# A decoder layer on one core: Wo behind the attention product, LayerNorm statistics behind v, row copies among the carries, expert gathers one by one, another order of the weight split

## The chip, the cores and the metric

One core of a Trainium2 chip runs the whole kernel in one launch. The metric is device time in microseconds (us), lower is better; times given are medians of several executions.

## The reference, cut to what matters

Input `x` is 16 sequences of 128 rows of 256 numbers. Three sublayers follow each other, each `x = x + f(LayerNorm(x))`:

```python
# 1: gated linear attention, 8 heads of 128; q, k normalised to length 1, alpha = sigmoid(x Wg)
S = a_t[..., None] * S + k_t[..., None] * v_t[:, :, None, :]     # one step of 128
o_t = einsum('bhkv,bhk->bhv', S, q_t)                             # then o @ Wo
# 2: cross attention to ctx: softmax(x (ctx W^T)^T) ctx
# 3: mixture of 8 experts, chosen per sequence (top 2 by the mean over its rows)
h = gelu(einsum('bsd,bkcd->bksc', x, Wd) + bd) * top_w            # Wd = down_w[top_i]: a gather
out = einsum('bksc,bkdc->bsd', h, Wu) + (top_w * bu).sum(1)
```

## The kernel before, in words

The 16 sequences are four groups `i` of four. A **unit** `n = 8 i + h` is the attention of one head `h` for one group, so there are 32 units. The recurrence over 128 steps is replaced by seven levels of a doubling scheme: `decay` (VectorE) and `carry` (ScalarE) make the operands of level l from those of level l-1, TensorE multiplies them (`levels`, in three runs: levels 0 and 2; 1, 3 and 4; 5 and 6), `keep` (VectorE) and `expand_*` (ScalarE) put the results into `attnT`, `attend` multiplies by v, `attend_transposed` turns the result, and `output_projection` adds it times Wo into an accumulator. Projections use float32 split into two parts, so `project` has three matmuls where one would do; the split of each weight is a cast on ScalarE and a subtraction on VectorE at the start (`split_weights`). Norms of q and k are sums of squares by 64 tiny matmuls (`norms`), floored by VectorE (`norm_floor`), raised to -1/2 by GpSimd (`reciprocal_norms`) and applied in `v_scaled` and `o_scaled`.

Sublayers 2 and 3 of group i-1, the **tail**, are woven into the units of group i. Each engine runs a list written out by hand; `tail_part(n, place)` puts a tail step at a head h and at a place in the unit. On TensorE the places are S (start), A (behind the second run of levels) and B (behind `attend`). On VectorE they are early, late, mid and end; on ScalarE early, mid and end. LayerNorm is `ln_variance` (VectorE), `ln_power` (GpSimd), `ln_normalize` (VectorE, writes `xn`), and then transposes of `xn` on TensorE: x2T for sublayer 2, x3T for sublayer 3, xT for the attention of the next group. Projections, v, o, transposes and tail products all go through four PSUM banks used in a fixed cycle (`ring`): a product waits until the one four places earlier has been read. The three long stretches in which tail and attention run together (units 8 to 15, 16 to 23, 24 to 31) are called passes 1, 2 and 3 here, units 0 to 7 pass 0. After unit 31 the tail of the last group runs by itself, in two halves.

Engines wait for each other by semaphores only; each engine works strictly in its own order, so a wait holds up all that is behind it. GpSimd also issues the four gathers of the chosen experts' weights (`fetch_experts`, one for each sequence of a group).

## Time and profile before

| | us |
|---|---|
| median of 3 runs | 564.17 (562.89 to 567.42) |
| profiled execution, its own time | 563.17 |
| its span | 561.4 |
| TensorE matmuls busy | 488.9 (87%) |
| VectorE busy | 383.1 (68%) |
| ScalarE busy | 356.9 (64%) |
| GpSimd busy | 85.1 (15%) |

The span is what the trace covers; the run's own time is 1.8 us longer. The granted clock of TensorE is a share of its full rate: 1.0 is 2.4 GHz, 0.5 is 1.2 GHz.

### The profile page before, as it was taken

What the parts mean: (1) busy time and instruction counts of PE and PEld (TensorE: products, weight loads), DVE (VectorE), ACT (ScalarE), POOL (GpSimd) and SP (SyncE); (2) the same over time, 40 slices, a digit from 0 to 9 for tenths busy, and PEclk for the clock granted to TensorE, in tenths of its full rate; (3) what the DMA queues carried; (4) which work ended last, traced back from release to release, by engine and by line L of the source; (5) the groups of instructions that cost most, each with busy time, mean ns of one, the idle gap of its engine ahead of it and who ended that gap; (6) DMA issues with size and microseconds to landing.
All of it is one profiled execution on the core that took longest, in us unless ns stands there. A gap on an engine that the chain in (4) does not pass through costs nothing. (4 is left out here: it accounts for less than half of the span.)

```text
span 561.4 us, 25935 instructions
## 1 busy us (share of the span) xinstructions
PE 488.9 (87%) x11232; PEld 407.4 (73%) x11232; DVE 383.1 (68%) x1069; ACT 356.9 (64%) x825; POOL 85.1 (15%) x71
## 2 busy tenths in 40 slices
PE   1798999999988999899988999899988999775616
PEld 1587888888877888787867888688867887664415
DVE  4588887766786888765686887765775888614541
ACT  4667787766758677567758677577748676442202
POOL 1012111111111111410111111410111111300020
PEclk9999999999999999899999999899989999997557
DMA  8800000001010100210010100210000100201021
GB/s 334 252 3 5 4 4 4 4 4 40 4 41 2 41 4 4 77 41 22 23 40 5 40 4 4 78 40 22 23 2 4 40 5 4 78 0 39 0 75 37
DMA packets 15264, 20.35 MB, mean 36 GB/s; under 512 B 1200, under 2 KB 12976, under 8 KB 15152
## 3 DMA queue, kind: packets, MB, share of 16 engines
q1 hardware_dynamic: 13872, 14.49, 7.6%
q0 software_dynamic: 1280, 4.20, 2.6%
q8 instruction: 89, 1.46, 1.1%
q14 instruction: 23, 0.19, 0.1%
HBM read 16.60 MB, written 2.10 MB: 33 GB/s over the span
## 5 line engine op out<-in xcount | busy, mean ns | idle before, releaser
L438 ACT COPY states<-states 128x512 f32<-128x512 f32 (+1 forms) x160 | 94.6, 592 | 95.3 <-DVE states L646 88.6
L363 POOL TENSOR_TENSOR rnorm<-norm_sq,neg_half 128x8 f32<-128x8 f32 (+1 forms) x33 | 53.8, 1631 | 291.0 <-DVE norm_sq L686 291.0
L646 DVE TENSOR_TENSOR states<-states,spans 128x512 f32<-128x512 f32 x128 | 88.5, 691 | 12.2 <-DVE states L646 4.6
L1128 PE MATMUL acc<-wo_sb,oT_sb 128*128 128x256 f32 x256 | 63.8, 392 | 8.2 <-ACT oT_sb L465 8.2
L1030 PE MATMUL ring<-xnT,wk_sb 128*128 128x512 f32 x192 | 55.7, 429 | 8.9 <-DVE v_sb L695 6.0
L1043 PE MATMUL ring<-wv_sb,xnT 128*128 128x256 f32 x384 | 57.5, 302 | 0.6 <-DVE wv_sb L877 0.6
L1128 PEld LDWEIGHTS acc<-wo_sb,oT_sb 128*128 128x128 f32 x256 | 46.0, 189 | 15.3 <-ACT oT_sb L465 9.3
L1030 PE MATMUL ring<-xnT,wq_sb 128*128 128x512 f32 x192 | 53.1, 412 | 1.7 <-ACT rowsT L469 1.0
L677 DVE COPY_PREDICATED blocks<-owned,lo_bank 128x128 f32<-128x128 uint32 x128 | 38.5, 301 | 20.2 <-PE lo_bank L1053 14.8
L1043 PEld LDWEIGHTS ring<-wv_sb,xnT 128*128 128x128 f32 x384 | 50.9, 200 | 1.1 <-DVE wv_sb L877 0.7
L1030 PE MATMUL ring<-xnT,wg_sb 128*128 128x512 f32 x192 | 51.0, 402 | 0.0
L1030 PEld LDWEIGHTS ring<-xnT,wk_sb 128*128 128x128 f32 x192 | 36.1, 200 | 16.8 <-DVE v_sb L695 7.1
L1030 PEld LDWEIGHTS ring<-xnT,wq_sb 128*128 128x128 f32 x192 | 33.6, 188 | 9.2 <-ACT rowsT L469 1.4
L1030 PEld LDWEIGHTS ring<-xnT,wg_sb 128*128 128x128 f32 x192 | 35.0, 195 | 6.2 <-DVE xnT L749 0.2
L460 ACT COPY attnT<-blocks 32x128 f32<-32x128 f32 x128 | 37.4, 292 | 1.1
L1109 PEld LDWEIGHTS ring<-v_sb,attnT 128*128 128x128 f32 x256 | 33.0, 192 | 5.2 <-issue 4.3
L450 ACT COPY attnT<-hi_bank 32x64 f32<-32x64 f32 x128 | 26.0, 203 | 16.0 <-PE hi_bank L1100 8.5
L1109 PE MATMUL ring<-v_sb,attnT 128*128 128x128 f32 x256 | 33.8, 275 | 0.4 <-issue 0.4
L1100 PE MATMUL hi_bank<-ones,squares 128*32 128x1 f32 x2048 | 26.7, 173 | 7.8 <-issue 5.9
L1100 PEld LDWEIGHTS hi_bank<-ones,squares 128*32 128x32 f32 x2048 | 24.2, 110 | 10.1 <-issue 7.9
L663 DVE TENSOR_TENSOR spans<-spans 128x128 f32<-128x128 f32 (+3 forms) x128 | 28.4, 222 | 4.4
L1053 PE MATMUL lo_bank<-states 128*32 128x32 f32 x2048 | 29.6, 198 | 1.5 <-issue 1.5
(145 smaller groups left out, 852.4 us busy)
## 6 DMA issues: line engine op xcount, KB each, us to landing
x_buf<-x_dram SPq DMA_DIRECT2D x4, 512.0 KB, 4.2
ctxT_sb<-ctxT_dram SPq DMA_DIRECT2D x8, 256.0 KB, 3.4
ctx_sb<-ctx_dram SPq DMA_DIRECT2D x4, 512.0 KB, 4.8
out_dram<-x_mid SPq DMA_DIRECT2D x8, 256.0 KB, 2.1
states<-wk_dram SPq DMA_DIRECT2D x1, 1024.0 KB, 6.1
states<-wg_dram SPq DMA_DIRECT2D x1, 1024.0 KB, 8.1
states<-wq_dram SPq DMA_DIRECT2D x1, 1024.0 KB, 10.1
v_sb<-wv_dram SPq DMA_DIRECT2D x1, 1024.0 KB, 11.7
```

The costliest lines, as they stand in the source:

```text
L363: nc.gpsimd.tensor_tensor(rnorm[:, m % 4, first:last], norm_sq[:, first:last], neg_half[:, first:last], ALU.pow).then_inc(rnorm_set, 1)
L438: nc.scalar.copy(dst, src).then_inc(carry_set, 1)
L460: last = nc.scalar.copy(attnT[lo:lo + BLOCK, :, lo:lo + BLOCK], blocks[lo:lo + BLOCK])
L646: nc.vector.tensor_tensor(dst, src, by, ALU.mult).then_inc(decayed, 1)
L663: nc.vector.tensor_tensor(spans[:, span_at(l):span_at(l) + m], view(src, off, [[2, m]]), view(src, off + 1, [[2, m]]), ALU.mult).then_inc( ...
L677: nc.vector.copy_predicated(blocks[:].rearrange("p b t -> p (b t)"), owned[:, mask].bitcast(U32), of_bank[:, N_IN * at:N_IN * at + N_IN]). ...
L1030: last = mm(dst[:], w[:, a, c, P * h:P * h + P], xnT[:, i % 2, b, c], start=(c == 0 and k == 0), stop=(c == KC - 1 and k == 2))
L1043: last = mm(dst[:, 2 * P * k:2 * P * k + 2 * P], xnT[:, i % 2, a, c, T * b:T * b + T], wv_sb[:, w, c, 2 * P * pair:2 * P * pair + 2 * P], ...
L1053: last = mm(dst[BLOCK * r:BLOCK * r + BLOCK, to:to + BLOCK], left[:, at:at + BLOCK], right[:, at:at + BLOCK], start=True, stop=True)
L1100: last = mm(hi_bank[BLOCK * r:BLOCK * r + BLOCK, to:to + 1], squares[:, a, at:at + BLOCK], ones[:], start=True, stop=True)
L1109: last = mm(dst[:, P * b:P * b + P], attnT[:, b], v_sb[:, n // 2 % 2, b, n % 2], start=True, stop=True)
L1128: last = mm(accs[z][:, D * m:D * m + D], oT_sb[:, n % 2, T * b:T * b + T], wo_sb[:, h], start=(h == 0 and m == 0), stop=(h == H - 1 and m ...
```

## The change

On TensorE, in each unit, `output_projection(n - 2)` moves from before place A to behind `attend(n - 1)`; x3T moves from S of head 5 to B of head 4. On VectorE, `residual` moves from mid to end of head 1 (behind `o_scaled`), `ln_variance("mid")` from end of head 1 to early of head 2 (behind `v_scaled`), and `weigh_up` from head 7 to head 0 of the next group. On ScalarE, the copies of x2T and probsT move to a new place between carries 2 and 3, and those of x3T from early of head 5 to end of head 4. On GpSimd, the power for q and that for k become two instructions with a semaphore each, and the gathers of a group are issued one at a time: sequence 0 in unit h = 6, sequence 1 when `norms` of that unit is done, sequences 2 and 3 behind the first and the second run of levels of unit h = 7. At the start the order is k 0, g 0, q 0, k 1 instead of k 0, k 1, g 0, q 0, and a one-column copy (`warm`) stands ahead of the first cast.

```diff
-            if place == "S" and h == 5 and t >= 0:
+            if place == "B" and h == 4 and t >= 0:
                 found = [("x3T", t, 0), ("x3T", t, 1)]
...
-            order = [("xT", 0, 0), ("xT", 0, 1), ("k", 0), ("k", 1), ("g", 0), ("q", 0)]
+            order = [("xT", 0, 0), ("xT", 0, 1), ("k", 0), ("g", 0), ("q", 0), ("k", 1)]
...
             def reciprocal_norms(m):
...
-                nc.gpsimd.tensor_tensor(rnorm[:, m % 4, first:last], norm_sq[:, first:last], neg_half[:, first:last],
-                                        ALU.pow).then_inc(rnorm_set, 1)
+                if m + 2 < U:
+                    nc.gpsimd.tensor_tensor(rnorm[:, m % 4, GB:2 * GB], norm_sq[:, GB:2 * GB],
+                                            neg_half[:, GB:2 * GB], ALU.pow).then_inc(rk_set, 1)
+                if m >= -1:
+                    nc.gpsimd.tensor_tensor(rnorm[:, m % 4, 0:GB], norm_sq[:, 0:GB], neg_half[:, 0:GB],
+                                            ALU.pow).then_inc(rq_set, 1)
...
             for n in range(U):
                 i, h = divmod(n, H)
+                if h == 7 and i > 0:
+                    pool.wait_ge(norm_mm, n + 2)
+                    fetch_experts(i - 1, (1,))
                 if 1 <= n:
                     reciprocal_norms(n - 1)
-                if h == 1 and i > 0:
+                if h == 2 and i > 0:
                     ln_power(("mid", i - 1))
...
                 if h == 6 and i > 0:
-                    fetch_experts(i - 1)
+                    fetch_experts(i - 1, (0,))
+                if h == 7 and i > 0:
+                    for run, b in ((RUNS[0], 2), (RUNS[1], 3)):
+                        pool.wait_ge(level_mm, LEVELS * n + DONE[run[-1]])
+                        fetch_experts(i - 1, (b,))
...
-                    if at == (2, "end"):
+                    if at == (2, "carry"):
                         for c in range(KC):
                             tail_to(rowsT[:, c], ("x2T", t, c), x2T_set)
                     if at == (3, "early"):
                         probs_out(t)
-                    if at == (3, "end"):
+                    if at == (3, "carry"):
                         tail_to(probsT[:].rearrange("p b t -> p (b t)"), ("probsT", t, 0), probsT_set)
-                    if at == (5, "early"):
+                    if at == (4, "end"):
                         for c in range(KC):
                             tail_to(rowsT[:, c], ("x3T", t, c), x3T_set)
...
-                if n + 1 < U:
-                    for l in range(1, INNER):
+                for l in range(1, INNER):
+                    if n + 1 < U:
                         carry(n + 1, l)
+                    if l == 2:
+                        tail_part(n, "carry")
                 tail_part(n, "end")
...
             act.wait_ge(consts_set, 1)
+            nc.scalar.copy(warm[:], neg_half[:, 0:1])
             split_weights(0)
             xT_upper(0)
             split_weights(1)
+            split_weights(2)
             k_out(0)
-            split_weights(2)
+            split_weights(3)
+            alpha_out(0)
+            q_out(0)
             k_out(1)
-            alpha_out(0)
-            split_weights(3)
-            q_out(0)
...
-                dve.wait_ge(rnorm_set, 2 * pair + 2)
+                dve.wait_ge(rk_set, 2 * pair + 2)
...
-                dve.wait_ge(rnorm_set, n + 2)
+                dve.wait_ge(rq_set, n + 1)
...
+                if at == (0, "late") and i >= 2:
+                    weigh_up(i - 2)
-                    if at == (1, "mid"):
+                    if at == (1, "end"):
                         residual(t)
-                    if at == (1, "end"):
+                    if at == (2, "early"):
                         ln_variance(("mid", t), x_mid)
...
-                    if at == (7, "late"):
-                        weigh_up(t)
...
             norm_floor(-2)
+            span_products(0)
             split_weights(3)
-            span_products(0)
...
                 if n < U:
                     levels(n, RUNS[1])
-                if n >= 2:
-                    output_projection(n - 2)
                 if n < U:
                     tail_part(n, "A")
                 if n >= 1:
                     attend(n - 1)
+                if n >= 2:
+                    output_projection(n - 2)
                 tail_part(n, "B")
```

TensorE around place A of head 2 (`L1128` before and `L1147` now are Wo, `L1137` and `L1156` the transposes of `xn`, `L1109` and `L1128` now `attend`). Before:

```order
L1053 MATMUL hi_bank<-states 32x32 x32
L1053 MATMUL lo_bank<-states 32x32 x16
L1128 MATMUL acc<-wo_sb,oT_sb 128x256 x4
L1137 MATMUL ring<-ident,xn 128x128 x8
L1109 MATMUL ring<-v_sb,attnT 128x128 x4
```

And now:

```order
L1072 MATMUL hi_bank<-states 32x32 x32
L1072 MATMUL lo_bank<-states 32x32 x16
L1156 MATMUL ring<-ident,xn 128x128 x8
L1128 MATMUL ring<-v_sb,attnT 128x128 x4
L1147 MATMUL acc<-wo_sb,oT_sb 128x256 x4
```

Wo stood between the levels and the transposes, and now stands behind the attention product.

VectorE from the end of unit h = 1 into unit h = 2. Before:

```order
L719 TENSOR_TENSOR x_mid<-acc,x_buf 128x512 x2
L710 TENSOR_TENSOR o_sb<-ring,rnorm 128x512
L612 BN_STATS stats<-x_mid 128x6 x4
L607 MEMSET scratch 128x1
L617 BN_AGGR mean_var<-stats 128x2 x4
L620 TENSOR_SCALAR var_eps<-mean_var 128x4
L686 TENSOR_SCALAR norm_sq<-hi_bank 128x8
L677 COPY_PREDICATED blocks<-owned,hi_bank 128x128 x2
L646 TENSOR_TENSOR states<-states,spans 128x2x16x16
L653 TENSOR_TENSOR states<-states,spans 128x4x32 x2
L695 TENSOR_TENSOR v_sb<-ring,rnorm 128x512
```

And now:

```order
L728 TENSOR_TENSOR o_sb<-ring,rnorm 128x512
L737 TENSOR_TENSOR x_mid<-acc,x_buf 128x512 x2
L704 TENSOR_SCALAR norm_sq<-hi_bank 128x8
L692 COPY_PREDICATED blocks<-owned,hi_bank 128x128 x2
L661 TENSOR_TENSOR states<-states,spans 128x2x16x16
L668 TENSOR_TENSOR states<-states,spans 128x4x32 x2
L713 TENSOR_TENSOR v_sb<-ring,rnorm 128x512
L627 BN_STATS stats<-x_mid 128x6 x4
L622 MEMSET scratch 128x1
L632 BN_AGGR mean_var<-stats 128x2 x4
L635 TENSOR_SCALAR var_eps<-mean_var 128x4
```

The statistics are computed behind the scaling of v; nothing was added or taken away.

GpSimd in heads 6 and 7 of pass 1, with the semaphores that each waits for. Before:

```order
L363 TENSOR_TENSOR rnorm<-norm_sq,neg_half 128x8 [waits v_set,o_set,norm_sq_set] x2
L370 DMA sel<-expert_dram,row_idx 128x513 [waits idx_set]
L370 DMA sel<-expert_dram,row_idx 128x513 x3
```

And now:

```order
L374 DMA sel<-expert_dram,row_idx 128x513 [waits idx_set]
L374 DMA sel<-expert_dram,row_idx 128x513 [waits idx_set,norm_mm]
L364 TENSOR_TENSOR rnorm<-norm_sq,neg_half 128x4 [waits v_set,o_set,norm_sq_set]
L367 TENSOR_TENSOR rnorm<-norm_sq,neg_half 128x4
L374 DMA sel<-expert_dram,row_idx 128x513 [waits idx_set,level_mm] x2
```

Four gathers in a row have become four that each wait for a point of TensorE's list.

## Rows read from the trace of the kernel before

**Rows 1.** Windows: us; busy PE, PEld, DVE, ACT, POOL; clock; DMA share; GB/s.

```profile
27.70:150.00 122.30, 120.88 (x3254) 100.94 (x3255) 91.68 (x235) 89.41 (x213) 17.91 (x11) 0.99 0.03 8
150.00:270.00 120.00, 112.76 (x2623) 94.93 (x2625) 89.62 (x257) 83.63 (x196) 20.45 (x15) 0.99 0.10 30
```

**Rows 2.** TensorE's waits: who waited for whom, us in total, times, longest.

```profile
PE acc L1128 <- ACT oT_sb L465: 8.2, 8, 2.9
PE ring L1030 <- DVE v_sb L695: 6.0, 3, 2.0
PE hi_bank L1100 <- issue: 5.9, 13, 0.5
...
PE ring L1146 <- issue: 3.3, 3, 1.2
...
PE ring L1030 <- ACT rowsT L469: 1.0, 3, 0.5
PE ring L1163 <- ACT probsT L469: 1.0, 2, 0.5
```

**Rows 3.** Timeline of the start: start us, us, engine, line, [idle before <- releaser].

```profile
7.93 1.28 ACT L528 ACT_TABLE_LOAD   x1 [7.93 <-DMA states<-wk_dram]
9.23 1.90 ACT L528 CAST wk_sb<-states 128x2048 fp32r<-128x2048 f32 x1
...
25.33 2.29 DVE L877 TENSOR_TENSOR wv_sb<-v_sb,wv_sb 128x2048 fp32r<-128x2048 f32 x1 [2.33 <-ACT wv_sb L528]
...
27.68 2.93 PE L1043 MATMUL ring<-wv_sb,xnT 128*128 128x256 f32 x12 [0.63 <-DVE wv_sb L877]
```

**Rows 4.** Timeline of heads 1 and 2 of pass 1, three engines.

```profile
154.09 1.28 DVE L719 TENSOR_TENSOR x_mid<-acc,x_buf 128x512 f32<-128x512 f32 x2
156.01 1.39 DVE L612 BATCH_NORM_STATS2 stats<-x_mid 128x6 f32<-128x256 f32 x4
158.11 1.01 POOL L355 TENSOR_TENSOR rstd<-var_eps,neg_half 128x4 f32<-128x4 f32 x1 [13.04 <-DVE var_eps L620]
160.89 0.69 DVE L695 TENSOR_TENSOR v_sb<-ring,rnorm 128x512 f32<-128x512 f32 x1 [1.00 <-issue]
163.55 1.38 DVE L628 TENSOR_SCALAR xn<-x_mid,mean_var,rstd 128x256 f32<-128x256 f32 x4
166.06 1.04 PE L1137 MATMUL ring<-ident,xn 128*128 128x128 f32 x8
```

**Rows 5.** Timeline of head 3 of pass 1: the normalisation for the next group, and Wo.

```profile
180.97 1.38 DVE L628 TENSOR_SCALAR xn<-x_buf,mean_var,rstd 128x256 f32<-128x256 f32 x4
181.35 1.99 PE L1128 MATMUL acc<-wo_sb,oT_sb 128*128 128x256 f32 x8 [0.90 <-ACT oT_sb L465]
```

**Rows 6.** Timeline of head 3 of pass 0: the same two.

```profile
70.49 1.38 DVE L628 TENSOR_SCALAR xn<-x_buf,mean_var,rstd 128x256 f32<-128x256 f32 x4
70.98 2.00 PE L1128 MATMUL acc<-wo_sb,oT_sb 128*128 128x256 f32 x8
```

**Rows 7.** Timeline: the end of a unit without a gather beside it.

```profile
140.55 0.73 PE L1100 MATMUL hi_bank<-ones,squares 128*32 128x1 f32 x64
141.21 1.68 PE L1043 MATMUL ring<-wv_sb,xnT 128*128 128x256 f32 x12
```

**Rows 8.** Timeline: the end of unit h = 6 of pass 1, beside the gathers.

```profile
229.12 0.62 PE L1100 MATMUL hi_bank<-ones,squares 128*32 128x1 f32 x12
...
232.26 2.93 PE L1043 MATMUL ring<-wv_sb,xnT 128*128 128x256 f32 x12
...
234.99 1.82 PE L1030 MATMUL ring<-xnT,wg_sb 128*128 128x512 f32 x6
```

**Rows 9.** Windows of 1 us: columns as in the first group.

```profile
231.00:232.00 1.00, 0.51 (x26) 0.43 (x29) 0.87 (x6) 0.00 (x0) 0.41 (x1) 1.00 0.64 213
233.00:234.00 1.00, 1.00 (x7) 1.00 (x6) 0.10 (x1) 0.96 (x5) 0.00 (x0) 0.50 0.37 140
```

**Rows 10.** The chain that ended last: start us, us, what (the last gather of the kernel).

```profile
542.67 3.85 DMA sel<-expert_dram,row_idx
```

More of the change, by code:

```diff
@@ L357, in reciprocal_norms @@
             def reciprocal_norms(m):
-                first, last = (4 if m < -1 else 0), (8 if m + 2 < U else 4)
                 pool.wait_ge(norm_sq_set, m + 3)
@@ L362, in reciprocal_norms, with fetch_experts @@
                 positive(pool, v_set, m - 1)
-                nc.gpsimd.tensor_tensor(rnorm[:, m % 4, first:last], norm_sq[:, first:last], neg_half[:, first:last],
-                                        ALU.pow).then_inc(rnorm_set, 1)
-            def fetch_experts(t):
+                if m + 2 < U:
[4 more added lines that the diff above has]
+                                            ALU.pow).then_inc(rq_set, 1)
+            def fetch_experts(t, sequences):
                 pool.wait_ge(idx_set, t + 1)
                 positive(pool, out_set, 2 * t)
-                for b in range(GB):
+                for b in sequences:
                     nc.gpsimd.indirect_dma_start(
@@ L392, in _ @@
                                         ALU.pow).then_inc(half_rstd[z], 1)
-            fetch_experts(NG - 1)
+            fetch_experts(NG - 1, range(GB))
         @block.scalar
@@ L918, in _ @@
                 tail_part(n, "end")
+            tail_part(U, "late")
             for k in range(LO_KEPT, KEEPS):
@@ L1241, in _ @@
             project(wk_sb, ("k", 0)).then_inc(k_mm, 1)
-            project(wk_sb, ("k", 1)).then_inc(k_mm, 1)
-            norms(-2)
             pe.wait_ge(w_split, 2)
             project(wg_sb, ("g", 0)).then_inc(g_mm, 1)
+            norms(-2)
             pe.wait_ge(w_split, 3)
             project(wq_sb, ("q", 0)).then_inc(q_mm, 1)
+            project(wk_sb, ("k", 1)).then_inc(k_mm, 1)
             norms(-1)
```

10 lines of the change are left out of this document (7 added, 3 removed).

## The prediction

> **What bounds the kernel now.** I read the windows of the span first, then TensorE's waits, then the timeline where those waits stand. The reader is to see in the windows [rows 1] that TensorE is the bound: in pass 0 it works 120.9 of 122.3 us, so nothing on VectorE (91.7) or ScalarE (89.4) can matter there, while in a window of a pass with a tail it works 112.8 of 120.0. The 7 us between are the prize, three times. The list of waits [rows 2] says what they are: Wo waiting for ScalarE's copy of oT (8.2 us in 8 waits), project k waiting for a ring bank that VectorE's scaling of v frees (6.0 in 3), the norms matmuls stopping for nothing that the profile shows (5.9 in 13 pieces), scores for its row copies (3.3 in 3), and 1.0 each for the copies of x3T and probsT. Each of the five edits aims at one of these. The question for each is what is late next on an engine that works in order.
>
> **Start.** A table load of 1.28 stands ahead of the first cast, which starts at 9.23 [rows 3]; a tiny copy ahead of it takes the load to where ScalarE is idle anyway. The v projection of unit 0 starts at 27.68, right behind the subtraction for wv (25.33 to 27.6), before which VectorE waited 2.33 for the cast of wv. That cast now comes before alpha, so the wait goes, but VectorE now waits for alpha and does the span products first. Lower bound 1.3 (the table load alone), upper 1.28 + 2.33 = 3.6. Besides, that first v projection ran at half clock, 2.93 against 1.68 in steady state [rows 3, 7], behind a TensorE with gaps; starting with fewer gaps may save the 1.25. Bounds 1.3 and 4.9; I take **3.0**, in the middle, since neither part is excluded. All of it counts, because TensorE bounds pass 0.
> The Trainium skill, ScalarE: Activation LUTs, section What ACT_TABLE_LOAD costs, puts a switch at about 1.28 us of load plus 1.38 of drain. The cast here starts 0.02 behind the end of the load [rows 3], so no drain is seen; by the page the start would return 1.4 us more.
>
> **Pass 0, head 3.** Wo, 2.0 long, started at 70.98, and the normalisation that the transposes of place A need ended at 70.49 + 1.38 = 71.9 [rows 6]: Wo covered it. With Wo behind `attend`, the transposes come first and wait 0.9. Nothing gives it back: **-0.9**.
>
> **Head 2 of each pass.** Before, the statistics (from 156.01 until GpSimd's power at 158.11, 2.1 us) and then a wait of 1.00 behind that power put the scaling of v at 160.89 [rows 4]; k waited 2.0 for it. Now the residual (1.28) only changes places with `o_scaled`, and the scaling of v comes 2.1 + 1.0 earlier, at about 157.8: k's wait is gone. The split power helps here: q and k apart take 1.01 each (the row of four columns), and v needs the first alone. But the statistics are still to be done before x2T. From scaling v to normalising took 163.55 - 160.89 = 2.66; with the statistics between, normalising starts at 157.8 + 2.66 + 2.1 = 162.6 and ends at 164.0. TensorE finished its levels at 166.06 less one Wo of about 1.85, that is 164.2, and without k's wait would at 162.2. Place A, formerly behind Wo, now comes at once: x2T waits 1.8. So 2.0 are gained and 1.8 lost: a wait of the same size, for the same VectorE work, 6 us later. **+0.5** for the three.
>
> **Head 3 of passes 1 and 2.** x2T's row copies between the carries are ready before scores asks, 3.3 / 3 = 1.1 gained. TensorE finished its levels at 181.35 - 0.90 = 180.4 [rows 5], now 1.3 earlier, 179.1, and does probsT (0.4). The xT transposes then need `xn`, which is ready at 180.97 + 1.38 = 182.35 and is bound by ScalarE's and VectorE's own chain, not by TensorE: a wait of 2.8. Then transposes 0.9, `attend` 1.0, Wo 1.85: 186.1, where the old order came to 183.2 + 0.4 + 0.9 + 1.0 = 185.5 and then waited 0.5 for probsT. The gains of scores (1.1), Wo (0.9) and probsT (0.5) are all spent on this wait: **0**. Pass 3 has no next group, no xT, and keeps them: 1.1 + 0.9 + 0.3 = **+2.3**.
>
> **x3T** in place B of head 4 needs an `xn` that is ready, with Wo ahead of it; its three waits go: **+1.0**. ScalarE does the two copies before `expand_wide` instead of behind it, the same work where it waited for norms anyway.
>
> **Other Wo waits.** 8.2 less the three of 0.9 in head 3 is 5.5. The last (about 0.7) has nothing to hide behind; of the 2.9 the `attend` now ahead waits for ScalarE's blocks written just before, so only 0.5 comes back; the remaining 1.9 (ScalarE late after table loads) is hidden by `attend` and keys. **+2.4**.
>
> **Gathers.** Undisturbed, norms take 140.55 to 141.21, 0.7 us; beside the four gathers 229.12 to 232.26, 3.1 [rows 7, 8]. In the window of 231 TensorE works half the time while the DMA engines are 0.64 busy; at 233 its clock is 0.50, 1.2 GHz, and v takes 2.93 (v to g 2.73 against 1.5) and g 1.8 [rows 8, 9]. Cost: 2.4 + 1.2 + 0.3 = 3.9. Pass 2 is alike, and pass 3 has the 2.4 without the slow clock: 10.2. My reading: instructions are fetched by DMA, 64 tiny matmuls use them up fast, and gather packets delay them. One by one, gathers 1, 2 and 3 go out at points behind which TensorE has long matmuls; gather 0 still falls near the norms. I leave 0.5 a pass for it and 0.3 for short unit 31: **+8.4**, bounds 0 (the stalls have another cause, or follow the gathers) and 10.2.
> The Trainium skill, Runtime: NRT & Kernel Launch, section Instruction fetch mechanics, says that a sequencer refills itself in blocks of 16 KiB and that this is mostly hidden. By that rule the stalls were not fetches and spreading gathers would return nothing; that is the first rival.
>
> `weigh_up` goes from head 7 to head 0, where its product is needed only after `attend` and Wo; VectorE is 1.2 later with its carries there and waits for the up products afterwards anyway: 0.
>
> **Clock.** The new waits of 1.8 to 2.8 (five of them) can bring the half clock, as the 2.4 of scattered idling did; of the three old k waits of 2.0 I cannot exclude it either. One more event of 1.2: **-1.2**; bounds 0 and 5 x 1.5 = 7.5.
>
> **Sum.** 3.0 - 0.9 + 0.5 + 2.3 + 1.0 + 2.4 + 8.4 - 1.2 = 15.5. The profiled execution took 563.17 (span 561.4), 1.0 under the median of 564.17; 563.2 - 15.5 = 547.7, so **548**.
>
> **Rivals.**
> - *The norms' stalls stay.* For: their releaser is unnamed, and small ones occur elsewhere without gathers. Against: three bursts, each exactly at the gathers, the DMA share rising with them. Then 548 + 8.4 = 556. Chance 0.20.
> - *Cold waits.* Each long wait at place A halves the clock for some 3 us. For: the clock after the gathers [rows 9]. Against: k's three waits of 2.0 stand in windows whose mean clock is 0.99 [rows 1]. 548 + 6 = 554. Chance 0.09.
> - *Better*: the start's upper end, all gather stalls gone, no slow clock: 542. Chance 0.08.
> - *Slower: the last gather.* It is issued behind the second run of levels of head 7; TensorE then has keys, `attend` and Wo, about 1.7 + 1.0 + 1.85 = 4.6 us, before the transposes of the gathered weights, and all of TensorE is queued behind these. From issue to landing the last gather took 3.85 [rows 10], so it fits by 0.7. Beyond 4.6 each us costs 3 (three passes); from 9.8 us on the change is slower than before, and at 12 it is 548 + 22 = 570. For: the gather shares GpSimd with the powers. Against: 3.85 was measured right behind three others. Chance 0.04.
> - *The edits do little*, because waits fall on other engines that I took for slack: 560. Chance 0.04.
>
> My forecast has 0.55, within 545 to 551. The range **541 to 558** takes in the upper end of the start, the full 10.2 for gathers, and the first two rivals, with about 0.1 left out. About 1% (558.5 to 569.8) is what a measurement can tell from no change: faster 0.88, same 0.08, slower 0.04.
>
> **What would show it.** k's waits of 2.0 gone and waits of some 1.8 before x2T, 2.8 before xT in passes 1 and 2, 0.9 in pass 0; norms beside gathers under 1.3 us and no clock of 0.5 there; v of unit 0 near 25; Wo's waits under 1.5 in all. The forecast is wrong if the norms still take 3 us, if the gathered weights' transposes wait, or if the xT waits cost more than they were given.

## The result, and the profile after

The changed kernel takes 547.26 us (median of 4 runs, 546.16 to 547.89) beside 563.53 of the kernel before (median of 4, 561.87 to 567.42): ratio 0.970, 95% interval 0.9646 to 0.9753. Its profiled execution took 546.16, its span 544.4. The forecast was 548, range 541 to 558.

The windows of the changed kernel, in the columns of [rows 1]; the first is most of pass 0, the second nearly pass 1, the last is what follows unit 31's attention:

```profile
24.00:146.00 122.00, 119.35 (x3253) 98.36 (x3254) 90.64 (x231) 89.16 (x212) 21.89 (x21) 1.00 0.04 10
146.00:266.00 120.00, 116.84 (x2793) 97.93 (x2795) 91.80 (x265) 87.39 (x206) 23.33 (x23) 0.99 0.10 30
482.00:544.00 62.00, 31.96 (x125) 25.38 (x124) 22.36 (x80) 10.29 (x24) 6.67 (x8) 0.68 0.12 34
```

Of the 7.2 us that TensorE idled in such a window of a pass, 3.2 are left. TensorE's waits, in the columns of [rows 2]:

```profile
PE ring L1156 <- DVE xn L643: 18.9, 7, 9.7
...
PE ring L1128 <- issue: 2.6, 2, 2.3
PE hi_bank L1119 <- issue: 2.0, 3, 1.3
PE hi_bank L1072 <- DVE blocks L692: 1.5, 1, 1.5
...
PE acc L1147 <- ACT oT_sb L477: 0.7, 1, 0.7
```

The waits of Wo for oT fell from 8.2 to 0.7, those of k for the scaled v are gone, the norms' stops fell from 5.9 to 2.0. Of the 5.9, 5.1 stood beside the gathers; the 2.0 all lie in pass 0, where there is no gather. In their place the transposes of normalised rows (L1156) wait 18.9, of which 9.7 is the start of the kernel and was there before: 9.2 us of waits are new. Their rows, of pass 0 head 3, then heads 2 and 3 of passes 1 and 2, and head 2 of pass 3:

```profile
67.46 1.09 PE L1156 MATMUL ring<-ident,xn 128*128 128x128 f32 x8 [0.83 <-DVE xn L643]
...
159.96 1.85 PE L1156 MATMUL ring<-ident,xn 128*128 128x128 f32 x8 [1.78 <-DVE xn L643]
...
178.59 1.09 PE L1156 MATMUL ring<-ident,xn 128*128 128x128 f32 x8 [1.38 <-DVE xn L643]
...
280.43 1.09 PE L1156 MATMUL ring<-ident,xn 128*128 128x128 f32 x8 [1.39 <-DVE xn L643]
...
298.35 1.09 PE L1156 MATMUL ring<-ident,xn 128*128 128x128 f32 x8 [2.00 <-DVE xn L643]
...
400.38 1.09 PE L1156 MATMUL ring<-ident,xn 128*128 128x128 f32 x8 [1.78 <-DVE xn L643]
```

Heads 1 and 2 of pass 1, which answer to [rows 4]: v is scaled straight behind the two powers, and the statistics follow it.

```profile
153.95 0.68 DVE L713 TENSOR_TENSOR v_sb<-ring,rnorm 128x512 f32<-128x512 f32 x1
154.55 1.39 DVE L627 BATCH_NORM_STATS2 stats<-x_mid 128x6 f32<-128x256 f32 x4
156.65 1.11 POOL L356 TENSOR_TENSOR rstd<-var_eps,neg_half 128x4 f32<-128x4 f32 x1 [2.27 <-DVE var_eps L635]
158.53 1.38 DVE L643 TENSOR_SCALAR xn<-x_mid,mean_var,rstd 128x256 f32<-128x256 f32 x4
```

And the end of head 6 of pass 1, which answers to [rows 8, 9]: the norms run through, v takes 1.70, and the clock is full. In the window of 224 the one gather that is under way keeps the DMA engines 0.54 busy, and 84 small matmuls run.

```profile
224.56 0.73 PE L1119 MATMUL hi_bank<-ones,squares 128*32 128x1 f32 x64
225.22 1.70 PE L1062 MATMUL ring<-wv_sb,xnT 128*128 128x256 f32 x12
225.59 1.00 POOL L374 DMA_INDIRECT sel<-expert_dram,row_idx  x1 [2.75 <-PE hi_bank L1119]
```
```profile
224.00:225.00 1.00, 1.00 (x84) 0.83 (x85) 0.79 (x2) 0.71 (x2) 0.00 (x0) 1.00 0.54 218
```

To see where time came from I compare the start of each unit's v projection, which every kernel does once a unit. By how much it is earlier than in the profile of the kernel before (27.68 for unit 0, 482.47 for unit 31, end at 561.4):

| | u0 | u2 | u10 | u14 | u16 | u22 | u24 | u26 | u28 | u30 | u31 | end |
|---|---|---|---|---|---|---|---|---|---|---|---|---|
| changed | 3.0 | 4.4 | 3.8 | 4.6 | 8.4 | 10.5 | 14.3 | 14.6 | 18.3 | 18.3 | 22.1 | 17.0 |
| start alone (s1) | 3.0 | 3.0 | 2.8 | 2.8 | 2.7 | 2.7 | 2.6 | 2.4 | 2.3 | 2.3 | 2.4 | -1.0 |
| gathers in a row again (g1) | 3.0 | 3.1 | 2.5 | 4.0 | 3.6 | 4.1 | 3.7 | 3.9 | 7.6 | 7.6 | 8.6 | 6.1 |
| Wo first in heads 2, 3 (h1) | 3.1 | 4.8 | 4.6 | 6.1 | 9.9 | 12.0 | 15.9 | 16.0 | 18.7 | 18.7 | 22.5 | 17.2 |
| and exp behind alpha (p1) | 3.0 | 3.4 | 3.2 | 6.2 | 9.9 | 13.5 | 17.5 | 17.8 | 21.5 | 21.7 | 25.5 | 20.0 |

The changed kernel gains 3.8, 3.9 and 3.8 in the three stretches with gathers (u14 to u16, u22 to u24, u30 to u31), 3.7 in heads 2 and 3 of pass 3, and gives 5.1 back behind u31. Four of the runs below that keep the old start (d1, d2, g2, n1) also have u0 0.3 earlier than the profile of the kernel before, so a difference of 0.3 at u0 is not the work of an edit.

### The profile page after: what moved, and what is told of

Read it like the earlier page. It is cut to its first block and busy times, and to the rows that moved or that the text cites. A ratio compares the mean times of both kernels' runs of the same rounds, so it can differ in the third digit from the quotient of the medians.

```text
span 544.4 us, 25975 instructions
## 1 busy us (share of the span) xinstructions
PE 483.6 (89%) x11232; PEld 399.9 (73%) x11232; DVE 380.4 (70%) x1069; ACT 355.6 (65%) x826; POOL 96.9 (18%) x102
## 3 DMA queue, kind: packets, MB, share of 16 engines
q8 instruction: 89, 1.46, 1.1%
## 5 line engine op out<-in xcount | busy, mean ns | idle before, releaser
L450 ACT COPY states<-states 128x512 f32<-128x512 f32 (+1 forms) x160 | 94.6, 591 | 91.0 <-DVE states L661 84.5
L364 POOL TENSOR_TENSOR rnorm<-norm_sq,neg_half 128x4 f32<-128x4 f32 x32 | 33.0, 1032 | 289.4 <-DVE norm_sq L704 289.4
L1147 PE MATMUL acc<-wo_sb,oT_sb 128*128 128x256 f32 x256 | 62.0, 386 | 0.7 <-ACT oT_sb L477 0.7
L1062 PE MATMUL ring<-wv_sb,xnT 128*128 128x256 f32 x384 | 54.5, 290 | 1.0 <-DVE wv_sb L895 1.0
L1049 PE MATMUL ring<-xnT,wk_sb 128*128 128x512 f32 x192 | 53.6, 415 | 1.7 <-DVE xnT L767 1.6
L1147 PEld LDWEIGHTS acc<-wo_sb,oT_sb 128*128 128x128 f32 x256 | 47.4, 195 | 6.2 <-ACT oT_sb L477 0.9
L1062 PEld LDWEIGHTS ring<-wv_sb,xnT 128*128 128x128 f32 x384 | 48.0, 188 | 1.5 <-DVE wv_sb L895 1.1
L1049 PEld LDWEIGHTS ring<-xnT,wk_sb 128*128 128x128 f32 x192 | 34.7, 193 | 8.4 <-issue 1.9
L1128 PE MATMUL ring<-v_sb,attnT 128*128 128x128 f32 x256 | 36.9, 289 | 2.8 <-issue 2.6
L1049 PEld LDWEIGHTS ring<-xnT,wg_sb 128*128 128x128 f32 x192 | 33.9, 189 | 6.8 <-DVE wg_sb L895 1.1
L1128 PEld LDWEIGHTS ring<-v_sb,attnT 128*128 128x128 f32 x256 | 32.9, 198 | 8.0 <-issue 6.9
L367 POOL TENSOR_TENSOR rnorm<-norm_sq,neg_half 128x4 f32<-128x4 f32 x32 | 33.4, 1044 | 3.2 <-DVE norm_sq L704 3.2
L722 DVE TENSOR_TENSOR state<-q_raw,alpha 128x512 f32<-128x512 f32 x32 | 22.1, 692 | 12.2 <-ACT q_raw L422 12.2
```

What stands on the lines that cost most here:

```text
L364: nc.gpsimd.tensor_tensor(rnorm[:, m % 4, GB:2 * GB], norm_sq[:, GB:2 * GB], neg_half[:, GB:2 * GB], ALU.pow).then_inc(rk_set, 1)
L367: nc.gpsimd.tensor_tensor(rnorm[:, m % 4, 0:GB], norm_sq[:, 0:GB], neg_half[:, 0:GB], ALU.pow).then_inc(rq_set, 1)
L450: nc.scalar.copy(dst, src).then_inc(carry_set, 1)
L1049: last = mm(dst[:], w[:, a, c, P * h:P * h + P], xnT[:, i % 2, b, c], start=(c == 0 and k == 0), stop=(c == KC - 1 and k == 2))
L1062: last = mm(dst[:, 2 * P * k:2 * P * k + 2 * P], xnT[:, i % 2, a, c, T * b:T * b + T], wv_sb[:, w, c, 2 * P * pair:2 * P * pair + 2 * P], ...
L1128: last = mm(dst[:, P * b:P * b + P], attnT[:, b], v_sb[:, n // 2 % 2, b, n % 2], start=True, stop=True)
```

## Experiments

They ran on three chips: g1, g2, w1, h1 on one, where the kernel before took 564.66; d1, s1, n1, p1 on a second (565.64); d2, g3, p2, r1 on a third (556.23). Ratios are to the kernel before on the same chip. The changed kernel wasn't run again beside them: its 547.26 belongs to the first measurement, with 563.53 before.

**g1: the gathers in a row again.** In the changed kernel:

```diff
-                if h == 7 and i > 0:
-                    pool.wait_ge(norm_mm, n + 2)
-                    fetch_experts(i - 1, (1,))
...
                 if h == 6 and i > 0:
-                    fetch_experts(i - 1, (0,))
-                if h == 7 and i > 0:
-                    for run, b in ((RUNS[0], 2), (RUNS[1], 3)):
...
+                    fetch_experts(i - 1, range(GB))
```

> The changed kernel with one edit undone: GpSimd issues the four expert gathers in a row again, behind the powers of head 6. Theory (the gathers' traffic stops TensorE's norms matmuls and is followed by the half clock): the norms of the unit behind head 6 take about 3 us again, v and g run at 1.2 GHz in passes 1 and 2, each of the units 14 to 16, 22 to 24 loses some 3.8 us, and the time is 547.3 + 8.4 to 11 = 556 to 558. Rival (the stalls belong to the norms and to the place, not to the gathers; the changed kernel lost them through its other edits): norms stay at 0.7 us, time 547, within 1.

Measured: 557.56, ratio 0.9877 (0.9803 to 0.9952), against 0.970 for the change in the first measurement: 1.8%, 10 us, and the intervals don't touch. On g1's own chip w1 and h1 below, both with the spread gathers, took 549.46 and 547.22. The table has it in the three stretches, where the gain of 3.8 becomes a loss of about 0.4 in the first two and a gain of 1.0 in the third; so of the 3.8 in the third only 2.8 belong to the gathers. Norms and v at the end of head 6 of pass 1:

```profile
225.15 0.28 PE L1111 MATMUL hi_bank<-ones,squares 128*32 128x1 f32 x12
225.80 0.24 PE L1111 MATMUL hi_bank<-ones,squares 128*32 128x1 f32 x3 [0.38 <-issue]
226.59 0.23 PE L1111 MATMUL hi_bank<-ones,squares 128*32 128x1 f32 x4 [0.55 <-issue]
227.28 0.24 PE L1111 MATMUL hi_bank<-ones,squares 128*32 128x1 f32 x4 [0.47 <-issue]
228.03 0.59 PE L1111 MATMUL hi_bank<-ones,squares 128*32 128x1 f32 x41 [0.50 <-issue]
228.54 2.35 PE L1054 MATMUL ring<-wv_sb,xnT 128*128 128x256 f32 x12
```

The norms come in pieces again, with pauses of about half a us between, and v is slow behind them. Theory held, at the upper end.

**g2: the gathers alone**, in the kernel before, with `weigh_up` in head 0 as it must be:

```diff
+                if h == 7 and i > 0:
+                    pool.wait_ge(norm_mm, n + 2)
+                    fetch_experts(i - 1, (1,))
...
-                    fetch_experts(i - 1)
+                    fetch_experts(i - 1, (0,))
+                if h == 7 and i > 0:
+                    for run, b in ((RUNS[0], 2), (RUNS[1], 3)):
+                        pool.wait_ge(level_mm, LEVELS * n + DONE[run[-1]])
+                        fetch_experts(i - 1, (b,))
...
+                if at == (0, "late") and i >= 2:
+                    weigh_up(i - 2)
...
-                    if at == (7, "late"):
-                        weigh_up(t)
```

> The kernel before with the gathers alone changed: one by one at the four points, and weigh_up in head 0 as a consequence. Theory: 3.9 us a pass return in passes 1 and 2, 2.4 in pass 3, less what the short last unit gives back: 563.5 - 8.4 = 555, between 552 and 557. Rival (the gain of the whole change is that of its waits, the gathers only move their stalls to levels and keys): 562 to 564, with idle pieces of no named releaser now in front of the levels of head 7.

Measured: 557.13, ratio 0.9859 (0.9787 to 0.9931): 8.0 us faster, between 3.9 and 12. The norms beside the first gather take 0.74, in a window in which the DMA engines are 0.65 busy, on the chip on which g1's are stopped at 0.47 to 0.79:

```profile
228.00:229.00 1.00, 1.00 (x55) 0.88 (x57) 0.83 (x2) 0.81 (x2) 0.00 (x0) 1.00 0.65 246
```

So one gather beside the norms doesn't stop them there; several behind each other do. Doing and undoing agree: this edit is half or more of the 16 us.

**d1: plain DMAs in pass 0.** Into the kernel before:

```diff
+                if n == 6:
+                    for b in range(GB):
+                        nc.gpsimd.dma_start(sel[:, b], expert[0:P, :]).then_inc(trial_in, 16)
```

> The kernel before, with four plain DMAs added in pass 0, where none were: GpSimd issues them behind the powers of unit 6, each 128 rows of 513 floats of the expert table, as many bytes as a gather, into the buffer of the gathered rows (overwritten later). Theory (any burst of DMA packets of this size beside the 64 small norms matmuls stops them, and the half clock follows): the norms behind unit 6 stretch from 0.7 to about 3 us with idle pieces of no named releaser, and v and g after them run at 1.2 GHz or nearly, 2.4 to 3.9 us in all. Rival (it is the indirect gather, its descriptors or GpSimd's work for them, that stops TensorE): the norms of unit 6 keep 0.7 us, the time moves by less than 0.5 us.

Measured: unit 7 starts 0.27 earlier than in the profile of before, no later. But the packets came later than I had planned: GpSimd issued them at 104.2 to 106.7, they landed by about 109, and so stood beside the second run of levels (96 tiny matmuls), not beside the norms. Windows of 1 us there:

```profile
107.00:108.00 1.00, 1.00 (x16) 0.55 (x18) 0.48 (x1) 0.73 (x2) 0.00 (x0) 1.00 1.09 390
108.00:109.00 1.00, 1.00 (x97) 0.96 (x96) 0.00 (x0) 1.00 (x2) 0.00 (x0) 1.00 0.75 283
```

97 small matmuls in one us with the DMA engines 0.75 to 1.09 busy, more than the 0.64 of [rows 9], and TensorE works on. A burst of plain packets beside the levels doesn't stop them; of the norms this run says nothing. In the same run its norms beside the real gathers were stopped as in the kernel before (6.1 us in 13 pieces).

**d2: plain DMAs beside the norms**, in four units of pass 0:

```diff
+                if 3 <= n < 7:
+                    positive(pool, trial_in, 16 * GB * (n - 3))
+                    pool.wait_ge(level_mm, LEVELS * n + DONE[RUNS[1][-1]])
+                    for b in range(GB):
+                        nc.gpsimd.dma_start(sel[:, b], expert[0:P, :]).then_inc(trial_in, 16)
```

> The kernel before, with four plain DMAs (as many bytes as the four gathers, from the same table into the same buffer, overwritten later) in each of the units 3 to 6 of pass 0, where none were. GpSimd waits for the second run of levels, so that they land beside and right behind the norms matmuls, as the gathers did, and not beside levels and projections as in the run with one burst. Theory (any burst of packets beside the norms stops them): four times the 2.4 of stopped norms, and the half clock with it: units 4 to 7 each 2.4 to 3.9 us later, together 10 to 15; the norms of these units take about 3 us. Rival (only indirect gathers stop TensorE): norms at 0.74 in all four, the time moves by under 1 us.

Measured: 558.04 beside 554.26 to 557.84 (median 556.23) of the kernel before there; unit 7 starts 0.26 later than in the profile of before. The norms of unit 6 stood in the burst and took 0.74. What I had not expected is the real gathers of this run, four in a row beside the norms of head 6, unchanged from the kernel before:

```profile
230.42 0.98 PE L1107 MATMUL hi_bank<-ones,squares 128*32 128x1 f32 x64
...
231.33 1.70 PE L1050 MATMUL ring<-wv_sb,xnT 128*128 128x256 f32 x12
```
```profile
230.00:231.00 1.00, 1.00 (x79) 0.88 (x78) 0.91 (x2) 0.76 (x2) 0.69 (x2) 1.00 0.79 222
```

0.98 instead of 3.1, with the DMA engines 0.79 busy, and v at full clock. In this pass the first gather went out 2.2 us ahead of the norms, and in [rows 8] 3.1, so the two are not quite alike. Pass 2 is the clean comparison: 2.9 ahead in both, and the norms take 0.74 where the kernel before needed 3.3:

```profile
352.66 0.74 PE L1107 MATMUL hi_bank<-ones,squares 128*32 128x1 f32 x64
```

In this profile of the third chip the stop isn't there in any pass: units 15, 23 and 31 start 2.2, 2.6 and 2.8 us earlier than just before these places. That is 7.6 us, and the kernel before, which wasn't profiled there, is 7.3 faster there than in the first measurement (556.23 against 563.53). So d2 can't tell whether plain packets would stop norms on a chip where gathers do.

**g3: four in a row, but behind the norms of head 6.** In the changed kernel, all four issued where the second is:

```diff
                     pool.wait_ge(norm_mm, n + 2)
-                    fetch_experts(i - 1, (1,))
+                    fetch_experts(i - 1, range(GB))
...
-                if h == 6 and i > 0:
-                    fetch_experts(i - 1, (0,))
-                if h == 7 and i > 0:
-                    for run, b in ((RUNS[0], 2), (RUNS[1], 3)):
...
```

> The changed kernel with the four gathers in a row, all of them behind the norms of head 6, where the changed kernel issues its second. Theory place (only the 64 tiny norms matmuls are hurt; behind them stand v and g of 1.7 and 1.5 us): norms at 0.73, no pieces without a releaser, time as the changed kernel, 547.3 within 1.5; the powers of the unit come 5 us later behind the gathers on GpSimd, which costs v's scaling and with it 2 to 4 us if it is not hidden. Theory dose (four in a row fill the DMA engines for 5 us, and what runs behind, v, g and the first levels of 96 small matmuls, stops too): pieces without a releaser before the levels of head 7, the half clock, 552 to 557.

Measured: 545.93, ratio 0.9825 (0.9768 to 0.9881), on the third chip. No piece without a releaser stands in levels, and from u3 to u30 it keeps within 0.6 us of the changed kernel's pace. The dose does no harm there, and GpSimd's powers behind the four are hidden. Since that chip doesn't stop norms either, this run doesn't decide place against dose. What speaks for dose is g2: with the place kept and one gather instead of four there was no stop.

**w1: Wo back ahead of place A**, in the changed kernel:

```diff
+                if n >= 2:
+                    output_projection(n - 2)
                 if n < U:
                     tail_part(n, "A")
                 if n >= 1:
                     attend(n - 1)
-                if n >= 2:
-                    output_projection(n - 2)
```

> The changed kernel with the output projection back ahead of place A in every unit. Theory (Wo, 1.85 us of work that waits for nothing but oT, covered the normalisation that x2T and xT need): the waits of 1.78, 1.39 and 1.78 before x2T and of 0.83, 1.38 and 2.00 before xT shrink to at most 0.3 each (9.2 us go), waits for oT of 0.9 in head 3 and of about 0.5 in head 1 come back, with up to 2.9 in two places behind table loads (6 to 7 us come): 545, between 543 and 547. Rival (the move behind the attention product is worth the 2.4 and more that its waits say, since x2T's waits are set by VectorE and only shift): 549 to 551.

Measured: 549.46, ratio 0.9724 (0.9657 to 0.9791), 2.2 us more than the change by the medians and 1.3 by the ratios, which is inside the interval. All waits for `xn` but the first are gone (9.2 us), and Wo waits 11.7 us in 12 places instead of 0.7 in one, 1.5 in each head 3. The rival was nearer.

**h1: Wo ahead of place A in heads 2 and 3 alone**, so that each place gets the order without the visible wait. In the changed kernel:

```diff
+                wo_first = n % H in (2, 3)
+                if n >= 2 and wo_first:
+                    output_projection(n - 2)
                 if n < U:
                     tail_part(n, "A")
                 if n >= 1:
                     attend(n - 1)
-                if n >= 2:
+                if n >= 2 and not wo_first:
                     output_projection(n - 2)
```

> The changed kernel with the output projection ahead of place A in heads 2 and 3 alone (there place A transposes freshly normalised rows), behind the attention product elsewhere. Theory: the nine us of waits for xn go but for 0.9 a pass for oT in head 3, and no wait for oT comes back in the other heads: 547.3 - 4.9 - 0.8 = 541.6, between 540 and 544, and the half clock behind x2T in pass 1 goes as well. Rival (the transposes of xT wait for VectorE's and ScalarE's own chain; what is gained in head 2 is waited out in head 3): head 3 waits 1.7 longer in three passes, 546 to 547.

Measured: 547.22, ratio 0.9703 (0.9634 to 0.9772): nothing of the 5.7 I expected. The two waits that have come up in head 3 of pass 1:

```profile
171.50 0.66 PE L1135 MATMUL ring<-ident,o_sb 128*128 128x128 f32 x4 [1.22 <-ACT probs L491]
...
176.10 1.99 PE L1147 MATMUL acc<-wo_sb,oT_sb 128*128 128x256 f32 x8 [1.55 <-ACT oT_sb L477]
```

TensorE comes to head 3 earlier and waits there for the bank that ScalarE's exp frees, and then for oT, which ScalarE copies only after two table loads, exp, alpha, blocks and q. Passes 2 and 3 have the same two waits (0.67 and 1.54, 0.34 and 1.51). Head 3 is bound by ScalarE, near to what the rival said, though the waits stand at oT and not at the transposes of xT. ScalarE's rows there:

```profile
168.42 1.28 ACT L491 ACT_TABLE_LOAD   x1
...
171.47 1.28 ACT L415 ACT_TABLE_LOAD   x1
172.76 0.60 ACT L415 ACTIVATE alpha<-ring 128x512 f32<-128x512 f32 x1
```

**p1: and exp behind alpha.** In h1, on ScalarE in head 3:

```diff
                 if n + 1 < U:
                     alpha_out(n + 1)
+                tail_part(n, "alpha")
...
-                    if at == (3, "early"):
+                    if at == (3, "alpha"):
                         probs_out(t)
```

> The kernel with Wo ahead of place A in heads 2 and 3, and besides ScalarE's exp of the scores behind alpha instead of ahead of it in head 3. Theory B (ScalarE's chain bounds head 3): alpha, and with it VectorE's span products and the decayed q, come some 3 us earlier; the two table loads stay but only one of them lies ahead of oT; oT's ring bank is freed 0.6 later (wait 1.8 instead of 1.2), the wait of 1.5 for oT shrinks; 547.2 - 1 to 4 = 543 to 546. Rival (the bank of the scores is what TensorE waits for, and it comes later): 547.2 + 2 = 549.

Measured: 542.46, ratio 0.9577 (0.9507 to 0.9647). The wait for oT is gone, that for the bank grew to 1.64:

```profile
173.36 0.66 PE L1136 MATMUL ring<-ident,o_sb 128*128 128x128 f32 x4 [1.64 <-ACT probs L491]
...
176.34 1.99 PE L1148 MATMUL acc<-wo_sb,oT_sb 128*128 128x256 f32 x8
```

Heads 2 and 3 of pass 1 (u10 to u12) take 33.3 instead of 34.8, those of pass 2 1.6 less, those of pass 3 1.0 less. By point value this beats both kernels; its interval and the changed kernel's touch (0.9647 and 0.9646), and they were not measured side by side.

**s1: the start alone**, in the kernel before; on ScalarE:

```diff
+            nc.scalar.copy(warm[:], neg_half[:, 0:1])
             split_weights(0)
...
+            split_weights(2)
             k_out(0)
-            split_weights(2)
-            k_out(1)
-            alpha_out(0)
             split_weights(3)
+            alpha_out(0)
             q_out(0)
+            k_out(1)
```

> The kernel before with the start of the change alone (the tiny copy ahead of the first cast, the other order of casts, subtractions and first projections). Theory: v of unit 0 starts near 24.7 instead of 27.68 and unit 1 is 3.0 us earlier, 4.3 where the clock stays full through the first v projection; it stays through the whole of the run, 563.5 - 3.0 to 4.3 = 559 to 560.5. Rival (later stages are bound by their own chains or by loads and take the start's gain back): 562 to 563.5.

Measured: 564.49, ratio 0.9989 (0.9955 to 1.0023), the second theory by the time: a gain of more than 2.5 us lies outside the interval. By the trace a gain of 2.3 to 3.0 stands up to u31 and is lost behind it. There two stretches of half clock stand that the profile of before has not: Wo behind unit 31 (2.49 instead of 1.99, and `attend` next to it 1.92 instead of the usual 1.05), and four of the last products (1.06 instead of 0.59). The first of them:

```profile
497.92 2.49 PE L1130 MATMUL acc<-wo_sb,oT_sb 128*128 128x256 f32 x8 [2.86 <-ACT oT_sb L466]
```

The instructions there are those of the kernel before, and so is the wait ahead of them, 2.87 there. The total moves from run to run as well: the kernel before itself took 561.68 to 568.13 on that chip at clocks of 0.941 to 0.954, and s1 560.41 to 567.11.

**n1: the statistics behind v alone**, in the kernel before, with Wo still ahead of place A.

```diff
-                    if at == (1, "mid"):
+                    if at == (1, "end"):
                         residual(t)
-                    if at == (1, "end"):
+                    if at == (2, "early"):
                         ln_variance(("mid", t), x_mid)
...
-                if h == 1 and i > 0:
+                if h == 2 and i > 0:
                     ln_power(("mid", i - 1))
```

> The kernel before with the statistics behind the scaling of v alone (the residual behind o_scaled, the statistics in head 2, GpSimd's power one unit later); Wo stays ahead of place A. Theory A: the waits of 2.0 of k for v's scaling go, x2T waits 0.6 at most since Wo covers the normalisation, 1.4 to 2.0 a pass, 563.5 - 4 to 6 = 558 to 559.5. Theory B (from the run with Wo sorted by heads: head 3 is bound by ScalarE's chain of table load, exp, table load, alpha, blocks, q, oT, which begins with the scores): head 3 waits for the ring bank of the scores and for oT what head 2 gained, and the time is 562 to 564; idle pieces of about 1.2 and 1.5 stand in head 3.

Measured: ratio 0.9956 (0.9909 to 1.0002), 2.5 us; its profiled execution took 566.6, so I read places in it and not its sum. k's waits are gone; ahead of the scores of the three passes stands now:

```profile
169.55 2.44 PE L1146 MATMUL ring<-projT,rowsT 128*128 128x128 f32 x16 [2.19 <-issue]
...
297.01 3.50 PE L1146 MATMUL ring<-projT,rowsT 128*128 128x128 f32 x16 [1.30 <-issue]
...
423.67 1.62 PE L1146 MATMUL ring<-projT,rowsT 128*128 128x128 f32 x6 [2.43 <-issue]
```

5.9 us in all instead of 3.3: the scores wait longer for row copies that are still behind the carries. And in each pass TensorE runs at half clock behind that wait: the scores take 2.44, 3.50 and 3.61 instead of 2.02, and in pass 1 v behind them 2.90 instead of 1.66. In pass 1, head 2 is 0.7 shorter and head 3 1.2 longer, and the 1.2 are v at half clock (2.70 to g instead of 1.50). Against the 2.0 of k's wait stand 1.0 of longer wait for the scores and 1.6 of half clock. So the gain is handed on to the next late step, as in theory B, but the step is the scores and not oT's bank, and the larger part is lost to the clock behind it. Whether the longer wait brought the half clock this one profile can't say; it has it in all three passes.

**r1: the copies back**, in the changed kernel:

```diff
-            if place == "B" and h == 4 and t >= 0:
+            if place == "S" and h == 5 and t >= 0:
                 found = [("x3T", t, 0), ("x3T", t, 1)]
...
-                    if at == (2, "carry"):
+                    if at == (2, "end"):
...
-                    if at == (3, "carry"):
+                    if at == (3, "end"):
...
-                    if at == (4, "end"):
+                    if at == (5, "early"):
```

> The changed kernel with the row copies undone: x2T's and probsT's copies behind all carries again, x3T in place S of head 5 with its copies early in head 5. By my terms (1.1 in pass 3, 1.0 for x3T, and in passes 1 and 2 nothing, since xT's normalisation is the later one): 547.3 + 2.1 = 549.4, waits of 1.1 before the scores in all three passes, and 0.3 to 0.5 before g for the row copies. Rival (the scores start the chain over max, exp, table loads and oT that bounds head 3, so that each 1.1 counts in all three passes): 547.3 + 3.3 + 1.0 = 551.6. Second rival (hidden anyway): 547.3.

Measured: 544.13, ratio 0.9798 (0.975 to 0.9846), on the third chip, where the changed kernel wasn't run. By the trace passes 1 and 2 lose nothing (0.2 and 0.3 ahead at u16 and u24) and pass 3 1.5, where 2.1 were expected in all. The scores wait 0.46, 0.41 and 0.62, less than the 1.1 expected. In passes 1 and 2 the normalisation for xT then starts 26.3 us behind the unit's v projection, against 26.7 in pass 2 of the changed kernel, which fits copies among the carries holding up that chain by about 0.4. Most of pass 3's loss stands here, where cross waits 1.07 and starts right behind ScalarE's copy of probsT:

```profile
421.38 1.97 PE L1182 MATMUL ring<-ctx_sb,probsT 128*128 128x256 f32 x8 [1.07 <-issue]
```

**p2: choice_weights one head later**, in p1:

```diff
-                    if at == (6, "end"):
+                    if at == (7, "end"):
                         choice_weights(t)
```

> The best kernel so far (Wo ahead of place A in heads 2 and 3, exp behind alpha) with VectorE's choice_weights behind o_scaled of head 7 instead of head 6. Theory (in the last unit VectorE's eight small instructions, 463.34 to 464.99 in the changed kernel, stand ahead of norm_floor and of the kept blocks, for which TensorE waits 1.54): that wait shrinks to 0.2 or less, 1.4 us are gained once; passes 1 and 2 do not move, since TensorE has keys of 1.9 ahead of the same blocks there or waits for others: 542.5 - 1.4 = 541. Rival (the same instructions now delay unit 0 of the next pass, where weigh_up stands behind them): 542.5 to 545.

Measured: 538.04, ratio 0.9694 (0.9644 to 0.9745), third chip. TensorE's wait for the kept blocks in unit 31 fell from 1.54 to 1.20 only:

```profile
462.02 0.76 PE L1073 MATMUL hi_bank<-states 128*32 128x32 f32 x64 [1.20 <-DVE blocks L693]
```

A miss: VectorE's lateness there has more causes than the eight small instructions. Its 538 is the lowest time of all, but up to u31 it stands 0.4 behind p1; its lead lies behind u31 (78.5 us to the end, p1 84.5), where r1 on the same chip also needs 78.5.

## Why the prediction was right, point by point

The total was right, 15.5 forecast and 16 measured, and the largest term, the gathers, came from the edit that it was given to. That the sum came so close is luck in part. In the profiled executions the change is 22.1 us ahead at u31, 6.6 more than forecast: 3.1 more in the gathers' stretches, 1.7 in the rest of passes 1 and 2, 1.4 at the start, 0.4 in the rest of pass 3 (the terms without a place of their own spread evenly over the passes). Then 5.1 are given back behind u31, for which the sum had 0.3.

- **Start**, +3.0 of bounds 1.3 to 4.9: v of unit 0 begins at 24.72, 3.0 earlier, of which 0.3 isn't the edit's (see under the table of v projections). The first cast starts at 7.69 instead of 9.23: 1.28 for the table load and 0.24 because its weights landed earlier. The further 1.4 up to u2 is the clock. The same start runs in g1 and w1, where unit 1 begins 1.3 later than in the changed kernel; the clock in the window 24 to 30 was 1.00 in the changed kernel and 0.72 in those and in s1. So it isn't given by the order of the work. The edit is worth about 2.7 up to u31; that it shortens the whole kernel by so much is not shown, since s1's runs leave at most 2.5.
- **Pass 0, head 3**, -0.9: the wait is 0.83.
- **Head 2**, waits of 1.8 before x2T: 1.78, 1.39, 1.78. The argument that one wait replaces another of its size held, and n1 and h1 show why: in n1 the order without Wo's move hands it to the scores and to a half clock behind them, in h1 covering x2T hands it to ScalarE's chain in head 3.
- **Head 3**, 2.8 before xT: 1.38 and 2.00. Mis-sized, and the step that was off is that `xn` is bound by ScalarE's and VectorE's own chain and not by TensorE. In pass 2 its normalisation starts 26.73 us behind the unit's v projection, and in the kernel before 27.37: the chain came 0.6 earlier when TensorE did. g1, whose three engines do the same work there, has 26.80 in pass 1 and a wait of 1.99. In pass 1 of the changed kernel the transposes of x2T and `attend` lost 1.6 at half clock (1.85 and 1.92 instead of 1.09 and 1.05). Beside g1, TensorE came 1.3 later and the normalisation 0.7 later (27.49), which makes the wait 1.38. That it starts 3.8 earlier than in [rows 5], as the unit itself does, is two effects that cancel. Passes 1 and 2 gained 0.8 and 1.5 from u10 to u14 and from u18 to u22, where 0.5 was forecast (0.17 for head 2, 0.33 for x3T); pass 3 gained 3.7 from u26 to u28, where 2.5 were; most of that excess is under Clock.
- **x3T**, +1.0: its waits are gone, and r1, which undoes the edit, has 0.46 and 0.45 of them in passes 1 and 2.
- **Other Wo waits**, +2.4, for the whole move less 0.9 in pass 0: w1 puts the whole move at 1.3 (ratios) to 2.2 (medians), where 1.5 were forecast; in its trace undoing it costs nothing in pass 1, 1.5 in pass 2 and 2.3 in pass 3. Right in sign, and too small to be fixed by these runs.
- **Gathers**, +8.4 of bounds 0 to 10.2: 10 us by undoing, 8.0 by doing alone, on chips that stop the norms. In the traces doing it alone gives 3.3, 3.4 and 2.8 in the three stretches, and undoing it takes 4.2, 4.2 and 2.8. The place was right and the size somewhat low: the 0.5 a pass kept for gather 0 wasn't needed (the norms beside it take 0.73 and 0.75), and pass 3 gave 2.8 where 1.6 was put. My reading of the cause, instruction fetches held up by gather packets, was not shown. In the DMA view instruction packets are seen for themselves, of 16 KiB, mostly one each 4 to 6 us here. Between 226 and 233.5, which holds all the pauses of [rows 8], none is recorded, and the norms had started again at 231.74, two us before the next. In pass 2 one is recorded at 356.3, among the pauses (355.0 to 357.7). Their places neither show the reading nor exclude it. The first rival, no gain, fell. The Trainium skill, Runtime: NRT & Kernel Launch, section Instruction fetch mechanics, from which I had derived it, says that crossing a 16 KiB boundary costs little and is mostly hidden. The runs don't contradict that, since nothing shows that the stops are fetches.
- **Clock**, -1.2: a half clock followed x2T's wait in pass 1 (transposes 1.85 instead of 1.09), and not the same waits in passes 2 and 3. One event, as taken, but by chance. The kernel before had one as well, which I overlooked: my argument that k's waits stand in windows with a mean clock of 0.99 [rows 1] covered only the one of pass 1. Behind the one of pass 3 k ran at half clock, 2.74 instead of 1.66:

```profile
412.80 2.74 PE L1030 MATMUL ring<-xnT,wk_sb 128*128 128x512 f32 x6 [1.96 <-DVE v_sb L695]
```

  With that wait the half clock is gone too, 1.1 on k alone, which is most of the 1.2 that pass 3 gained beyond the forecast. Between these waits the balance is one stretch new and one less, so the term of -1.2 has no counterpart there.
- **Not in the sum: 5.1 us given back behind u31.** Unit 31 projects nothing for a next unit, so VectorE and the gathers are closer to TensorE. Its rows in the changed kernel:

```profile
465.74 0.76 PE L1072 MATMUL hi_bank<-states 128*32 128x32 f32 x64 [1.54 <-DVE blocks L692]
...
467.70 0.56 PE L1072 MATMUL lo_bank<-states 128*32 128x32 f32 x20 [0.46 <-issue]
468.19 3.24 PE L1197 MATMUL ring<-ctxT_sb,xw_sb 128*128 128x512 f32 x4
...
480.50 1.61 PE L1128 MATMUL ring<-v_sb,attnT 128*128 128x128 f32 x8 [2.31 <-issue]
481.90 3.13 PE L1147 MATMUL acc<-wo_sb,oT_sb 128*128 128x256 f32 x8
```

  3.2 are lost up to the transposes of the gathered weights (2.0 for `o_sb` and blocks; stops of 0.8; keys at half clock 1.4; against a stop of 1.45 that the kernel before had), the rest is half clock, in Wo and in the last products. On the third chip g3 and r1 need 80.2 and 78.5 us from u31 to the end where the changed kernel needs 84.0 and the kernel before 78.9, so most of it belongs to the run or the chip; r1, with the same wait for the blocks (1.46), has no stop and no half clock in unit 31 and is 0.3 behind the kernel before at those transposes.

**What stays open:** why norms stop beside several indirect gathers on two of the chips and not on the third; whether plain packets would do it where gathers do; what the changed kernel takes on the third chip. There the gain by the gathers should be near zero, since there is nothing to remove, and of r1, the nearest kernel that ran, 2.0% is left. That is 12 us by the medians, where the forecast without the gathers has 7.1; which terms give more there no run separates.

## What to carry to other kernels

A wait that one edit removes is worth only what the next late step leaves: covering 5 us of waits in head 2 gave nothing until ScalarE's table loads in head 3 were taken off the path to oT. So before moving work, follow the freed time to the next engine that is late, and look there for what begins with TensorE's own products and moves with them. Bursts that stop an engine without a named releaser can be a property of the chip: measure before and after on the same one.

## What the runs showed of the hardware

- Four indirect gathers of 256 KB in a row beside 64 tiny matmuls make these take 3.2 us instead of 0.73 on two chips, with pauses of 0.3 to 0.55 (in [rows 8] matmuls in runs of 12, 10, 4 and 38, in g1 12, 3, 4, 4 and 41). On a third chip the same took 0.74 to 0.98 without a pause. One gather alone beside them cost nothing on a chip where four stopped them (g2, 0.74). The DMA engines' busy share doesn't decide: on that chip 0.47 to 0.79 with stops (g1) and 0.65 without (g2).
- Each stretch of half clock costs 1 to 2 us, and it falls on the same instructions in one run and not in another (unit 0's v and g: 1.70 and 1.56 in the changed kernel, 2.93 and 1.82 in g1).
- An indirect gather of 128 rows holds GpSimd 0.94 to 1.42 us. A power of 128x4 mostly takes 1.01, one of 128x8 1.64 to 1.71, so splitting one into two costs GpSimd about 0.4 and gives the first half 0.65 earlier.
